# A counting sort inside a graph network kernel: a table of its own for each half of a step, and two bf16 products in place of one fp32 product

## The reference, cut to what matters

```
edge_index = jnp.stack([src, dst])
h = jnp.maximum(_layernorm(x, axis=-1), 0.0)
x = x + _L0_gnn_ref(h, edge_index, edge_weight, ...)      # hypergraph attention, 2 inner layers
h = ...;  x = x + _L1_gnn_ref(h, edge_index, ...)         # message MLP, segment_sum over dst
h = ...;  x = x + _L2_gnn_ref(h, src, dst, ...)           # gated messages, segment_sum over dst
h = ...;  x = x + _L3_gnn_ref(h, edge_index, ...)         # GAT forward and backward
```

## Time and profile before

| | us |
|---|---|
| median of 3 runs | 11423.58 (11420.74 to 11429.36) |
| the profiled execution | 11428.81 |
| its span, first to last instruction | 11427.0 |
| PE busy in the span | 8042.8 (70%) |
| DVE busy | 7905.9 (69%) |
| POOL busy | 7501.8 (66%) |
| ACT busy | 5676.6 (50%) |

### The profile page before, as it was taken

How to read it: one execution, slowest core, us unless ns; L and a number is a source line. 1 busy time by engine, 2 the same in 40 slices (tenths; PEclk the granted TensorE clock), 3 DMA queues, 4 the chain that set the end, 5 groups by cost and what they waited for, 6 DMA issues and landing times. The chain is left out here.

```text
span 11427.0 us, 187407 instructions
## 1 busy us (share of the span) xinstructions
PE 8042.8 (70%) x47078; PEld 5923.8 (52%) x47078; DVE 7905.9 (69%) x33260; ACT 5676.6 (50%) x17089; POOL 7501.8 (66%) x7674
## 2 busy tenths in 40 slices
PE   7895777666665777666645555888888777767776
PEld 5674444444444444444434555666666444444444
DVE  8766888744447888644453222588886799979998
ACT  4553555454444555455551111366665566646665
POOL 2444777677775777677756777466663677747775
PEclk8776666655556666555557777899998666666666
DMA  1112222255652222488954444355553544444443
GB/s 17 9 20 50 55 55 55 65 136 135 136 127 56 56 55 55 126 215 212 211 140 130 131 131 131 109 155 154 154 153 100 136 139 138 138 116 139 139 137 114
DMA packets 713309, 1294.48 MB, mean 113 GB/s; under 512 B 197090, under 2 KB 369216, under 8 KB 711872
## 3 DMA queue, kind: packets, MB, share of 16 engines
q0 software_dynamic: 282368, 575.57, 24.7%
q1 hardware_dynamic: 389520, 612.10, 16.8%
q10 hardware_dynamic: 40368, 94.82, 2.1%
HBM read 1048.44 MB, written 233.37 MB: 112 GB/s over the span
## 5 line engine op out<-in xcount | busy, mean ns | idle before, releaser
L623 POOL DMA_INDIRECT WK<-tab,IDX x4640 | 4411.9, 951 | 1702.9 <-issue 1372.3
L1637 POOL DMA_INDIRECT B<-tab,IDX x1856 | 1780.2, 959 | 710.8 <-issue 529.2
L623 POOL DMA_INDIRECT H<-tab,IDX x928 | 880.2, 949 | 539.2 <-DVE H L1441 261.6
L1767 ACT ACTIVATE B<-B 128x33 f32<-128x33 f32 x5568 | 1210.7, 308 | 7.9
L1656 DVE TENSOR_REDUCE WK<-PS 128x4 f32<-128x1024 f32 x928 | 1130.3, 1219 | 91.7 <-PE PS L1782 85.2
L926 PE MATMUL PS<-B 128*128 128x130 f32 (+1 forms) x3712 | 777.7, 374 | 393.2 <-ACT B L899 393.1
L1815 PEld LDWEIGHTS PS<-B,H 128*128 128x128 f32 x3712 | 829.2, 333 | 377.5 <-issue 372.2
L1815 PE MATMUL PS<-B,H 128*128 128x132 f32 x3712 | 893.6, 435 | 177.3 <-DVE ACC L1669 177.3
L1782 PE MATMUL PS<-WK,B 27*128 27x512 bf16 x1856 | 690.0, 481 | 396.0 <-DVE WK L1656 386.7
L926 PEld LDWEIGHTS PS<-B 128*128 128x128 f32 x3712 | 661.8, 268 | 581.6 <-ACT B L899 581.6
L887 ACT ACTIVATE B<-PS,PICK 18x512 bf16<-18x512 f32 x464 | 357.3, 770 | 1138.2 <-PE PS L944 1116.3
(11 more groups left out here) (476 smaller groups left out, 19980.9 us busy)
## 6 DMA issues: line engine op xcount, KB each, us to landing
H<-onehots SPq DMA_DIRECT2D x232, 768.0 KB
B<-onehots SPq DMA_DIRECT2D x232, 384.0 KB
onehots<-B ACTq DMA_DIRECT2D x232, 384.0 KB
WK<-tab,IDX POOLq DMA_INDIRECT x4640
onehots<-WK SPq DMA_DIRECT2D x232, 256.0 KB
B<-onehots SPq DMA_DIRECT2D x232, 256.0 KB
WK<-onehots SPq DMA_DIRECT2D x232, 256.0 KB
onehots<-B SPq DMA_DIRECT2D x232, 128.0 KB
```

The lines of the kernel that those rows point to most:

```text
L623: po.indirect_dma_start(out=G[:, g % n, k, :], out_offset=None, in_=table, in_offset=bass.IndirectOffsetOnAxis(ap=IDX[:, idx, t:t + 1], ax ...
L1637: po.indirect_dma_start(out=eG[:, g % 5, k, :], out_offset=None, in_=tab[TW3], in_offset=bass.IndirectOffsetOnAxis(ap=IDX[:, o, t:t + 1], ...
L1767: i = ac.activation(eR[:, q, k, 33 * h:33 * h + 33], eG[:, g % 5, k, 33 * h:33 * h + 33], ACT.Copy, scale=eEX[:, r, 4 * k + h:4 * k + h + 1])
```

## The change

The zero fill, the scatter and the loads back work on two tables per order, `recd[o][q]`, one for each half q of a step, each with a semaphore of its own. A scatter now waits only for the scatter of the same half one step before. The loads back are four, and PE adds the two tables of an order up while it transposes them (32 matmuls per order in place of 16). In `tables_ve` five DVE instructions more cut `pk` into a multiple of 32 and the low 5 bits, each exact in bf16, and `rank_pe` adds them with two bf16 products in place of the fp32 product.

```diff
-        recd = [dram(f"pieces{o}", (PIECES + 128, 2 * SLOTS)) for o in range(2)]
+        recd = [[dram(f"pieces{o}_{q}", (PIECES + 128, 2 * SLOTS)) for q in range(2)] for o in range(2)]
...
             for o in range(2):
-                sp.dma_start(recd[o].rearrange("(p t) f -> p (t f)", p=128), idle).then_inc(s_fill, 16)
+                for q in range(2):
+                    sp.dma_start(recd[o][q].rearrange("(p t) f -> p (t f)", p=128), idle).then_inc(s_fill, 16)
...
-            ve.tensor_tensor(bt(pk), bt(tsum), pkb.unsqueeze(2).broadcast_to([CH, NB, TC]), ALU.add).then_inc(s_pk, 1)
+            own(ve, "ve", ve.tensor_tensor(bt(pk), bt(tsum), pkb.unsqueeze(2).broadcast_to([CH, NB, TC]), ALU.add))
+            own(ve, "ve", ve.tensor_scalar(pki, pk, 0.0, None, ALU.add))
+            ve.tensor_scalar(tsi, pki, SLOTS - 1, None, ALU.bitwise_and)
+            own(ve, "ve", ve.tensor_scalar(pki, pki, 5, 5, ALU.arith_shift_right, ALU.arith_shift_left))
+            ve.tensor_copy(pkp[0], pki)
+            ve.tensor_copy(pkp[1], tsi).then_inc(s_pk, 1)
...
-                mm = pe.matmul(out_, ident[0:CH, 2 * k + c:2 * k + c + 1].broadcast_to([CH, 128]), pk, start=False, stop=True)
+                pick_ = identb[0:CH, 2 * k + c:2 * k + c + 1].broadcast_to([CH, 128])
+                pe.matmul(out_, pick_, pkp[0], start=False, stop=False)
+                mm = pe.matmul(out_, pick_, pkp[1], start=False, stop=True)
...
-                        ac.wait_ge(s_sc[z // NP], 32 * (z % NP + 1))
+                        for q in range(2):
+                            ac.wait_ge(s_sc[z // NP][q], 16 * (z % NP + 1))
...
-                    if 2 * k + q >= 1:
-                        po.wait_ge(s_sc[o], 16 * (2 * k + q))
+                    if k >= 1:
+                        po.wait_ge(s_sc[o][q], 16 * k)
                     po.indirect_dma_start(
-                        out=recd[o], out_offset=bass.IndirectOffsetOnAxis(ap=ROWI[:, o, 2 * k + q:2 * k + q + 1], axis=0),
-                        in_=OUT[x % 4][:, 64 * q:64 * q + 64], in_offset=None, compute_op=ALU.add).then_inc(s_sc[o], 16)
+                        out=recd[o][q], out_offset=bass.IndirectOffsetOnAxis(ap=ROWI[:, o, 2 * k + q:2 * k + q + 1], axis=0),
+                        in_=OUT[x % 4][:, 64 * q:64 * q + 64], in_offset=None, compute_op=ALU.add).then_inc(s_sc[o][q], 16)
...
-            sp.dma_start(LD[o].rearrange("p (c f) -> p c f", c=8),
-                         recd[o][0:PIECES, :].rearrange("(c p k) f -> p c (k f)", p=116, k=4)).then_inc(s_rec[o], 16)
+            for q in range(2):
+                sp.dma_start(LD[o][q].rearrange("p (c f) -> p c f", c=8),
+                             recd[o][q][0:PIECES, :].rearrange("(c p k) f -> p c (k f)", p=116, k=4)).then_inc(s_rec[o], 16)
...
-            pe.wait_ge(s_rec[o], 16)
+            pe.wait_ge(s_rec[o], 32)
             for w in range(2):
                 for c in range(8):
-                    piece = LD[o].rearrange("p (c s w) -> p c s w", c=8, w=2)[:, c, :, w]
-                    mm = pe.matmul(PS[:, 4 * o + 2 * w + c // 4, 116 * (c % 4):116 * (c % 4) + 116], piece, ident[0:116, 0:116],
-                                   start=True, stop=True)
+                    for q in range(2):
+                        piece = LD[o][q].rearrange("p (c s w) -> p c s w", c=8, w=2)[:, c, :, w]
+                        mm = pe.matmul(PS[:, 4 * o + 2 * w + c // 4, 116 * (c % 4):116 * (c % 4) + 116], piece,
+                                       ident[0:116, 0:116], start=q == 0, stop=q == 1)
```

More of the change, by code:

```diff
@@ L224, in build @@
         UF, ONF = room(sort_area, 128), room(sort_area, 128)
+        pkp = [room([[LOW[0:CH, 0, :], 250 * i]], CW // 2).bitcast(BF16) for i in range(2)]
+        pki, tsi = (LOW[0:CH, 1, CW * i:CW * i + CW].bitcast(I32) for i in range(2))
         iob = room(sort_area, 25).bitcast(BF16)[:, 0:NB]
@@ L230, in build @@
         onec = room(sort_area, 1)
-        LD = [B2[0:116, 200 + 4200 * o:2248 + 4200 * o] for o in range(2)]
+        LD = [[B2[0:116, 200 + 4200 * o + 2100 * q:2248 + 4200 * o + 2100 * q] for q in range(2)] for o in range(2)]
         gi, gl, go = (WK[:, 1568 + NT * i:1568 + NT * (i + 1)].bitcast(I32) for i in range(3))
@@ L242, in build @@
         s_rank, s_v, s_q, s_slot, s_prod, s_ohd, s_oha, s_pm, s_ev = S.pt, S.va, S.e1, S.e2, S.p2, S.r, S.ex, S.ag, S.xa
-        s_sc = [sem(f"scattered{o}") for o in range(2)]
+        s_sc = [[sem(f"scattered{o}_{q}") for q in range(2)] for o in range(2)]
         s_rec = [sem("records0"), sem("records1")]
@@ L449, in place_ac @@
                         z = y - 4
-                        ac.wait_ge(s_sc[z // NP], 32 * (z % NP + 1))
+                        for q in range(2):
+                            ac.wait_ge(s_sc[z // NP][q], 16 * (z % NP + 1))
                     ac.activation(OUT[y % 4], PS[:, 4 + y % 2, 0:128], ACT.Copy).then_inc(s_ev, 1)
         def scatter_po(po):
-            po.wait_ge(s_fill, 32)
+            po.wait_ge(s_fill, 64)
             for x in range(2 * NP):
@@ L471, in ordered_sp @@
         def ordered_sp(sp, o):
-            sp.wait_ge(s_sc[0], 32 * NP)
-            sp.wait_ge(s_sc[1], 32 * NP)
-            sp.dma_start(LD[o].rearrange("p (c f) -> p c f", c=8),
-                         recd[o][0:PIECES, :].rearrange("(c p k) f -> p c (k f)", p=116, k=4)).then_inc(s_rec[o], 16)
+            for q in range(2):
+                sp.wait_ge(s_sc[0][q], 16 * NP)
+                sp.wait_ge(s_sc[1][q], 16 * NP)
+            for q in range(2):
+                sp.dma_start(LD[o][q].rearrange("p (c f) -> p c f", c=8),
+                             recd[o][q][0:PIECES, :].rearrange("(c p k) f -> p c (k f)", p=116, k=4)).then_inc(s_rec[o], 16)
         def blocks_pe(pe, o):
```

## The result

| | before | after |
|---|---|---|
| median of 20 runs each | 11421.62 (11404.97 to 11436.58) | 11435.98 (11424.39 to 11449.49) |
| ratio | | 1.0015, 95% interval 1.0008 to 1.0022 |
| the profiled execution | 11428.81 | 11445.85 |
| its span | 11427.0 | 11444.1 |
| mean granted clock of PE, share of 2.4 GHz | 0.688 | 0.673 |

The change makes the kernel 0.15% slower. The forecast of 11262, the range up to 11380 and the sign were all wrong. The stretches of the two orders and of the loads back say where to look; they answer to the earlier trace rows and the last row.

What follows compares the result with a forecast made beforehand. Bound: a POOL scatter chain of 7.4 us a step alternating with a slow PE of 10 us. Terms -52.2 - 100.4 - 11.9 + 4 - 28.7 + 25 = -164.2 took 11428.8 to 11264.6 us, named as 11262; range 11235 to 11380.

Steps and rivals of the forecast that it cites:

- Scatter: POOL's scatters in both orders: two in flight, landing still 3.2 us, POOL's need 3.1 us a step, within 5.36.
- Rival 2: Both orders: scatters don't overlap, the chain stays at 6.9 to 7.4 us a step, total about 11432; chance 0.05.
- Rank on PE: PE's steps: bf16 products shorten order 1's from 5.25 to 4.59 us, worth nothing while DVE leads.
- Rival 1: Both orders: PE's clock stays low, 306 us over the sum, 11568; chance 0.07 full, 0.20 mild (11290 to 11400).
- First order: Order 0, first to last step: 312.3 us in place of 364.5 at DVE's free pace, -52.2.
- Between the orders: From order 0's last step to order 1's row table: 12.5 us in place of 24.4, -11.9.
- Tables: Five more DVE instructions ahead of each order's steps: 2.0 us per order, +4, bounds +2 to +5.7.
- Tail: From order 1's last step to the loads back: 17.7 us in place of 46.4, -28.7.
- Zero fill: Two more zero fills at the start cost 0, as the first scatter comes 100 us later; uncovered some 10 us.
- Loads back: After the last scatter: two more loads on four of 16 DMA engines and doubled transposes, +25, bounds 0 to +35.
- Rival 3: Loads back cheaper through more engines or better overlap, 10 to 25 us off, 11240 to 11252; chance 0.06.
- The chances: Whole kernel: 0.88 faster, 0.05 within 0.2%, 0.07 slower; 0.62 for 11245 to 11285 us.

Runs made afterwards that it cites:

- the last experiment: Changed kernel with fp32 product back, order 0's loads back during order 1, 24 wide matmuls before each order's first step: 11243.51 us, ratio 0.9852.
- Experiment 1: Changed kernel with the fp32 product back and the five DVE instructions out, two tables kept: 11266.34 us, 0.9863 of the kernel before.
- 2: Kernel before with the two bf16 products in place of the fp32 one, one table per order: 11459.82 us, ratio 1.0036.
- 3: Changed kernel plus two unused bf16 matmuls of 392 columns in each step of order 1: 11272.38 us, 0.9868 of the kernel before.
- 5: Changed kernel plus three unused fp32 matmuls of 64 columns in each step of order 1: 11507.59 us, 1.0081 of the kernel before.
- 6: Changed kernel plus one unused bf16 matmul of 392 columns in each step of order 1: 11286.55 us, 0.9888 of the kernel before.
- the burst experiment: Changed kernel plus 24 unused bf16 matmuls of 392 columns once, ahead of order 1's steps: 11397.26 us, 0.9978 of the kernel before.
- experiment 8: Changed kernel with the fp32 product back and each load back cut to 96 and 80 partitions in place of 116: 11260.02 us, ratio 0.9863.

## Why the prediction was wrong, point by point

- **What bounds.** Right for the kernel before: the scatter chain and slow stretches of PE alternated. One row was misread: the placing of 5.87 us lies between 3.76 and 6.93, so the clock was not at 0.50 after the gap of 3.25 us but fell inside the placing. The free paces of 6.09 and 5.36 us were right as well, since the last experiment keeps them through both orders.
- **Scatter.** Right in what matters: both of a step in flight, landing 3.5 us against 3.2. Wrong in a size: a pair holds POOL 3.8 us in order 0 (1.69 + 2.12) and 3.7 in order 1 (2.18 + 1.55), not 3.1, still less than a step. Rival 2 is out.
- **Rank on PE: the step that failed.** The prices were right (8.68 us a step at low clock against 8.67, 0.33 us between bf16 starts). "While DVE leads this is worth nothing by itself; it is hidden behind DVE" was wrong. It took for granted that PE's clock is the same with and without those columns. At 1.2 GHz exchanging the product even saves 1.3 us a step, but it takes away work with which the clock came back in order 1. Experiment 1 has the clock back within 57 us of the first step, the changed kernel not in 433 us. Experiments 1 and 2 make it a 2 x 2 table: the bf16 parts cost 40 us with one table and 170 with two (11266.34 to 11435.98). 3, 5 and 6 show that one wide matmul a step repairs it and three thin ones don't. That the tables alone come within 5 us of the forecast of 11262 is in part luck: in their profile order 1 took 292.9 us and the loads back 69.8, where 275.1 and 63.4 had been forecast, and everything behind the sort, forecast as unchanged, was 17 us shorter than before.
- **Rival 1** had the mechanism and the price, at a chance of 0.07 for the full form and 0.20 for a mild one. Its evidence stood in the profile: once low in order 1, PE stayed low for 62 us though busy throughout. The prediction cited this, but weighed the gaps (1.04 us held, 3.25 us did not), and didn't ask what ended those 62 us. It also took about half of the steps of the kernel before to be low; by the PEclk of 0.85 and 0.74 it was 30% and 52% of the time of the two orders. In the burst experiment the placing in which the clock fell had a gap of 0.63 us before it, shorter than either. Of rival 1's two orders only order 1 came in full: it took 158 us more than forecast, and rival 1 had priced it at 155 of its 306 us.
- **First order.** 330.6 in place of 312.3. PE's clock was low until 133 us, then fell at 174, 239, 270, 335 and 365 us and came back each time, after 24 us or after 7. Only the low start and the three long stretches held DVE up: of its 51 gaps from step to step all but nine are 6.1 us, the others 6.95 to 9.34 (one from 189.13 to 198.35), together 21 us over the free pace. With the fp32 product, in the tables alone, PEclk was 0.96 in this stretch, not 0.81, and the order took 316.7.
- **Between the orders.** 16.2 us from the last L417 to L334 in place of 24.4, forecast 12.5. The 3.7 us are missing because PE's clock fell once more at 430 us, and its last two placings took 5.43 and 7.06 us.
- **Tables.** Right: L334 to the first L417 took 31.6 us in place of 29.8, +1.8 for the five new instructions, forecast 2.0.
- **Tail.** -20.5 in place of -28.7. With PE at 0.50 it still had three steps to place when DVE began its last one: they end 20.2 us after that L417, where 12.1 had been counted.
- **Zero fill.** Right at 0: the first scatter came at 113.0 us in place of 111.3, later only by the +1.7 of the tables.
- **Loads back.** Right: PE stopped waiting for the two pairs 24.1 and 45.9 us after the issue, forecast 24 and 45, and L531 began 57.9 us after it, forecast 57. The four-engine share of 0.27 held for the added loads, and experiment 8 shows it to be one of shape. Rival 3 is out for this kernel.
- **The chances.** 0.88 for faster rested on little. The forecast needed a clock above 0.95 in both orders, in a kernel whose profile showed 0.85 and 0.74, after a change that makes PE's steps leaner; the argument that DVE's lead would secure it was never backed by a row.

Left open: why one wide matmul more is enough where the six bf16 products of a step are not, and what in order 0 makes the clock fall and come back as it does. The counting matmuls (L319), two wide ones a step, stand only in order 0, and fit with experiment 3, but no run took them away. Nor is it settled why the 96-wide transposes stayed at 0.50 where the 116-wide ones gained the clock.

## What to carry to other kernels

Before taking work off PE, read the granted clock of the stretch and ask what brings it back after a fall: matmuls that look like a cost can be what holds 2.4 GHz, and an engine 99% busy in the profile can be at half its clock throughout. When a change has two parts, weigh each alone; here one was worth 154 us and the other lost nearly all of it. Where PE sits at 1.2 GHz although it never waits, one wide matmul for nothing per step is a quick test for whether the clock is the loss; here it was worth 149 us.

## What the runs showed of the hardware that was not expected

- PE busy 435.97 of 441 us and at 1.2 GHz all that time. The Trainium skill ("TensorE: Matmul & The Clock Gate", section "What's actually happening") says that a gate sets PE's clock by how busy PE has been lately. The trace does not bear this out if busy is read off the profile's rows: the same busy share came with 0.50 here and with 0.95 in the tables alone (265.00 of 265 us). What differed was the matmuls of a step, not how long PE was busy.
- The clock fell inside a placing in front of which PE had waited 0.63 us, about as in front of those before it (burst alone), while in the kernel before it had held through 1.04 us.
- Two scatters issued 0.30 us apart hold POOL longer than two alone, 3.7 to 3.8 us in place of 3.1, but not always the same one: in order 0 of the changed kernel the second takes 2.12 us, in order 1 the first 2.18 us. The cause was not looked for.
- Cutting a 116-partition load to 96 and 80 partitions took it from 87 to 230 GB/s.
